# A graph network's node-group rows in f32 instead of f16, and the masks compared from them

## What is computed

```python
h = jnp.maximum(_layernorm(x), 0.0)
x = x + _L0_gnn_ref(h, src, dst, ...)              # GCN: segment_sum of x[src] * norm
h = jnp.maximum(_layernorm(x), 0.0)
x = x + _L1_gnn_ref(h, edge_index, W1, b1, W2, b2) # relu(relu([x_i, x_j - x_i] @ W1 + b1) @ W2 + b2), segment_max
h = jnp.maximum(_layernorm(x), 0.0)
x = x + _L2_gnn_ref(h, edge_weight, ...)           # segment_sum(h[src] * weight) / degree, two linear maps
h = jnp.maximum(_layernorm(x), 0.0)
x = x + _L3_gnn_ref(h, edge_index, edge_type_8, ...)  # two relational convolutions: two passes over the edges
```

## Time and profile before

| | us |
|---|---|
| median of 3 runs | 10746.02 |
| lowest and highest | 10732.53, 10749.62 |
| the profiled execution | 10738.4 |
| its span | 10736.3 |

### The profile page before, as it was taken

The page is one execution under the profiler, slowest core; times in us unless marked ns, Lnnn a source line. Parts: engine busy times, 40 slices in busy tenths (PEclk is TensorE's granted clock), DMA queues, the critical chain, the costliest instruction groups (busy, mean ns, idle before and its releaser), DMA issues.

```text
span 10736.3 us, 132836 instructions
## 1 busy us (share of the span) xinstructions
PE 5143.0 (48%) x35468; PEld 3759.8 (35%) x35468; DVE 4481.7 (42%) x9066; ACT 1867.5 (17%) x5090; POOL 6455.6 (60%) x6245
## 2 busy tenths in 40 slices
PE   3788477667676557777777311111112321111111
PEld 3677455555555435555555111111111111111110
DVE  7898555555555554444444221121112121111112
ACT  0677223323333200000000100000000100000000
POOL 8234555555555546666565566666666566666666
PEclk9999778888877778889888655555555655555555
DMA  6000133333333212222222222222221222222222
GB/s 260 23 15 15 36 88 95 93 92 94 93 92 92 79 44 65 64 63 64 65 64 62 82 58 56 56 57 59 56 58 56 87 58 56 57 56 58 57 58 56
DMA packets 501320, 736.15 MB, mean 69 GB/s; under 512 B 142419, under 2 KB 217811, under 8 KB 498372
## 3 DMA queue, kind: packets, MB, share of 16 engines
q0 software_dynamic: 199616, 212.17, 9.4%
q1 hardware_dynamic: 174060, 258.01, 7.7%
q10 hardware_dynamic: 127584, 265.22, 6.5%
HBM read 429.83 MB, written 305.03 MB: 68 GB/s over the span
## 4 chain that ended last, share of the span: by engine, by line
another core or an unknown queue 37%; PE 23%; issue 18%; DVE 11%; POOL 4%; DVEq 3%; ACT 2%; SPq 1%; DMA 1%; ACTq 0%; POOLq 0%
PE ps L1674 11%; DVE scn L1330 3%; PE ps L1738 2%; PE ps L1706 2%; PE ps L1583 2%; PE ps L1550 1%; POOL big L723 1%; PE ps L1555 1%; DVE picked_nodes L1266 1%; DVE idx L1292 1%; POOL big L786 1%; PE ps L1723 1%; PE ps L1649 1%; SPq L591 1%
## 5 line engine op out<-in xcount | busy, mean ns | idle before, releaser
L776 POOL DMA_INDIRECT gat<-typed_table,idx x3128 | 2996.7, 958 | 1591.4 <-issue 905.8
L776 POOL DMA_INDIRECT gat<-node_table,idx x2689 | 2626.6, 977 | 1845.0 <-issue 887.0
L1674 PE MATMUL ps<-big 128*128 128x320 bf16 x13230 | 2313.5, 331 | 627.3 <-issue 317.7
L1738 PE MATMUL ps<-ident,scn 128*128 128x128 f32 x3136 | 873.0, 370 | 3566.9 <-DVE scn L1330 2409.7
L1330 DVE TENSOR_TENSOR_SCAN scn<-flags,scn,ps 128x256 f32<-128x256 bf16 x1176 | 873.5, 743 | 3518.1 <-remote 3257.7
L1738 PEld LDWEIGHTS ps<-ident,scn 128*128 128x128 f32 x3136 | 533.5, 213 | 3869.6 <-issue 3847.2
L1674 PEld LDWEIGHTS ps<-big 128*128 128x128 bf16 x13230 | 1405.2, 109 | 1306.3 <-issue 450.9
L862 ACT COPY dmp<-ps 128x256 f32<-128x256 f32 x1568 | 578.9, 369 | 6295.8 <-remote 3966.9
L1706 PE MATMUL ps<-ident,gat 128*128 128x128 f32 x3136 | 820.9, 355 | 501.3 <-DVE gat L1297 310.7
L1266 DVE SCALAR_TENSOR_TENSOR picked_nodes<-node_ids,nodes_in_groups,ps 128x320 f32<-128x320 f32 x441 | 240.0, 544 | 1297.9 <-remote 749.3
L1706 PEld LDWEIGHTS ps<-ident,gat 128*128 128x128 f32 x3136 | 473.3, 177 | 646.0 <-issue 588.7
(11 more groups left out here) (289 smaller groups left out, 6037.9 us busy)
## 6 DMA issues: line engine op xcount, KB each, us to landing
scan_rows<-dmp ACTq DMA_DIRECT2D x784, 256.0 KB
flags<-keep_and_type_rows SPq DMA_DIRECT2D x980, 128.0 KB
spread_table<-tsl ACTq DMA_DIRECT2D x101, 576.0 KB, 16.0
shared<-spread_table SPq DMA_DIRECT2D x196, 288.0 KB
gat<-typed_table,idx POOLq DMA_INDIRECT x3128
gat<-node_table,idx POOLq DMA_INDIRECT x2689
typed_table<-shared SPq DMA_DIRECT2D x20, 1280.0 KB
group_rows<-node_group_rows SPq DMA_DIRECT2D x196, 128.0 KB
```

Of the source, the lines that this page charges most:

```text
L776: nc.gpsimd.indirect_dma_start(gat[:, k, g // ST, g % ST, :], None, table[:, :], bass.IndirectOffsetOnAxis(ap=idx[:, k, g:g + 1], axis=0)) ...
L1674: last = nc.tensor.matmul(product_bank(q, n), masks[:, n % 2, a, :], x3p[:, t, a, :, :].rearrange("p d b -> p (d b)"), start=a == 0 and t ...
L1738: last = nc.tensor.transpose(bank(2 + b1)[:, g * P:g * P + P], by_edge(scn[:, b1, :], g), ident[:, :])
```

## The change

The rows of node groups are held in f32: the table in DRAM (`group_d`), the tile into which SP loads (`grows`), and the tile that is written to the table (`group_t`). `grp_id` stays f16 and the masks stay bf16. To make room, `grp` no longer has memory of its own but lies over `scn`, the scan buffer, which is first written in the MLP pass; `group_t` lies there too. No instruction is added, removed or moved on any engine; L884 becomes a copy from f32 to f32.

```diff
-    group_d = nc.dram_tensor("node_group_rows", [NS, P], f16).ap()
+    group_d = nc.dram_tensor("node_group_rows", [NS, P], f32).ap()
...
-        grp = sb("node_groups", [P, NS])
...
-        grows = sb("group_rows", [P, K, P], f16)
+        grows = sb("group_rows", [P, K, P])
...
-        group_t = scn[:, :, :].rearrange("p b n -> p (b n)")[0:NS // 4, 0:2 * P].bitcast(f16)
+        grp = scn[:, :, :].rearrange("p b n -> p (b n)")[:, 0:NS]
+        group_t = scn[:, :, :].rearrange("p b n -> p (b n)")[0:NS // 4, 0:4 * P]
```

## The result

The changed kernel takes **10,770.3 us** (median of 11 runs, 10,756.5 to 10,785.2) beside 10,756.2 us for the kernel before, run beside it (11 runs, 10,732.5 to 10,769.2): ratio **1.0019**, 95% interval 1.0011 to 1.0026. A repetition (after_again) gave 1.0015 [1.0005, 1.0025]. In one set of runs used further down (set 3), one of 21 executions of the kernel before took 18,755 us; it is left out of the ratios.

What follows compares the result with a forecast made beforehand. Both passes were held bound by engines waiting for each other. Terms 101 + 68 + 50 + 35 + 30 = 284 us, less 20, on 10738 gave 11002, as a median 11,010 us; 8-in-10 range 10,870 to 11,135.

Steps and rivals of the forecast that it cites:

- The mask's price: DVE's mask comparison in both passes: 1500 ns with one f32 operand, +0.69 us each, 441 times.
- All 147 MLP masks on the path, +101: MLP pass: every mask releases PE's product, so each added 0.69 us counts, 101 us.
- 98 turns of the weighted pass, +68: Weighted pass: 98 masks lie between pick and scaling while PE idles, 68 us; the other 196 cost nothing.
- I take off 20 us: Whole sum: 20 us absorbed where PE waits for fetches or 4 to 6 us stalls without known cause.
- The clock, weighted +50: Weighted pass: longer PE idle time turns some 30 product pieces slow, 1.7 us each, 50 us.
- The clock, MLP +35: MLP pass: longer PE idle time turns about 22 product pieces slow, 1.6 us each, 35 us.
- The load, +30: MLP pass: masks for position 4 wait for loads grown to 256 KB, 0.8 us each, 30 us.
- Held fetches, put at 0: Both passes: longer masks hold POOL's fetches, perhaps 120 us more POOL time, costing 0 because POOL has room.
- A: Rival: idle DVE hides half of 169 us, no clock reaction; +85, 10,830 us; chance 0.17.
- B: Rival: the mask keeps its rate, only the load changes; 0 to 30 us, 10,755 us; chance 0.05.
- C: Rival: mask as fast as now and lets go of POOL, 49 us of held fetches return; 10,700 us; chance 0.02.
- D: Rival: slow clock lasts (+85 more), loads lengthen stalls or show as size (+100); 11,190 us; chance 0.10.

Runs made afterwards that it cites:

- set 3: Third of five sets of follow-up runs, each with the kernel before run beside it; there the kernel before took 10,767 us.
- few_f32: Changed kernel with all fetches but one of each step left out in both passes; one run, MLP pass 2286 us, weighted pass 1681 us.
- twice_both: Kernel before, with one f16 instruction making each mask twice in both passes; ratio 1.048 to the kernel before.
- mask_only: Kernel before with `grp_id` in f32, so masks are long; rows f16, loads 128 KB; ratio 1.0073.
- wtd_again: Kernel before with f32 rows in the weighted pass alone, f16 masks in the MLP pass; ratio 1.0149, where signals were on time.
- load_only: Kernel before with loads doubled to 256 KB and f16 masks; ratio 1.0004.
- few: Kernel before with all fetches but one of each step left out in both passes, f16 masks; one run, MLP pass 1998 us, weighted pass 1661 us.
- mlp_only: Kernel before with f32 rows used in the MLP pass alone; ratio 1.0087.
- gap_both: Kernel before with small POOL memsets behind the fetches of some steps, 196 in the weighted and 147 in the MLP pass; ratio 0.9975.
- pad_hold: Kernel before with an extra DVE comparison of 512 elements from two SBUF operands ahead of each f16 mask; ratio 1.0077.
- set 4: Fourth of five sets of follow-up runs; signals were on time and the kernel before took 9,308.6 us.
- half: Kernel before with all fetches but two of each step left out in both passes, f16 rows; one run, MLP pass 2005 us, weighted pass 1662 us.
- thrice_wtd: Kernel before, with one f16 instruction making each mask three times in the weighted pass alone; ratio 1.0357.
- short_f32_wtd: Kernel before with f32 rows in the weighted pass alone, each mask there made for 5 of 10 node groups; 9,307.4 us.

## Why the prediction was wrong, step by step

- **The mask's price: right.** 1.50 forecast, 1.479 measured, by the slope between rows of mixed operands.
- **All 147 MLP masks on the path, +101: right as PE's idle time wherever signals are on time** (+110 in few_f32, +97 in twice_both), wrong where they are late (+44 in the changed kernel).
- **98 turns of the weighted pass, +68: the same.** +65 in few_f32; in the changed kernel PE's idle time fell by 46. Gaps of PE of 4 us and more went from 33 (194 us) to 12 (79 us), all other gaps of 0.6 us and more from 206 to 270 us. The +64 is there, and the stalls gave back 115. (In mask_only they gave back nothing, and the pass was shorter by its busy time.)
- **The failed step: "I take off 20 us"** for the stalls without a cause. The terms ahead of it add up to 284 and the change measured 14, so with these terms it should have been 270. Some 60 us of that are the clock and 30 the load, below; the largest part is waiting: 169 us forecast at the masks, -2 us of idle time measured. I had seen the stalls and priced them by feeling. A stall whose cause is unknown makes every added time uncertain by its whole sum; here about 365 and 606 us of late signals stood against 304 us of new work. The prediction had named this sign itself: if the mask is long and a pass does not grow, another wait had been the last one there.
- **The clock, weighted +50: wrong in its reason.** From the earlier trace rows I read that an idle time of 2.7 us makes the next product slow. In few_f32 the idle time is 2.72 us, and the product runs at 2.4 GHz:

```profile
4235.83 0.41 PE L1716 MATMUL ps<-ident,gat 128*128 128x128 f32 x2 [2.72 <-DVE gat L1307]
4236.07 2.21 PE L1684 MATMUL ps<-big 128*128 128x320 bf16 x15
```

  In the whole weighted pass PE's busy time fell by 46 us there, and rose by 32 in wtd_again. The single idle time ahead of a product does not set its clock; my sorting mixed it with the stalls further back.
- **The clock, MLP +35: right in sign, five to six times too small** where signals are on time (busy +178 in few_f32 and +215 in twice_both, granted clock 0.95 to 0.84 and 0.83). In the changed kernel it was +15, from 0.81 to 0.79; that much of the slow running was there already is my reading.
- **The load, +30: wrong, 0.** load_only gives +5 and -3. The wait for the load grows to 140 us with 128 KB loads too, once other waits are gone (140.3 in few, 141.1 in twice_both).
- **Held fetches, put at 0: probably wrong without late signals.** The size was near: the fetches of the changed kernel take 162 us more of POOL's time in the weighted pass and 6 in the MLP pass, for the 120 of the prediction. In wtd_again a fetch that begins inside a mask lasts 2.14 us, and DVE then waits for its rows:

```profile
4339.45 1.46 DVE L1263 TENSOR_TENSOR big<-group_rows,group_ids 128x1280 bf16<-128x1280 f32 x1
...
4339.59 2.14 POOL L782 DMA_INDIRECT gat<-node_table,idx  x1 [0.30 <-issue]
...
4343.25 0.23 DVE L1299 COPY idx<-src_i 128x4 int32 x1 [2.34 <-DMA gat<-node_table,idx]
```

  The fetch ends 0.82 us behind the mask, as the earlier trace rows had it. PE's idle time in this pass grows by 104 us, 65 by the turns as in few_f32, and I put the other 39 down to this. That last split is an inference from two runs.
- **The rivals.** A (+85) had the right direction for the right reason, that cover exists, and named DVE's idle time instead of the stalls. B's 0 to 30 us holds the measured 14, but by luck: its condition, a mask that keeps its rate, did not come true. C's fetches were held longer, not let go. D (+440) has the size that twice_both measured, +448, and in part the reason: slower matmuls are 237 us of it (D had 170), while the loads and the unexplained stalls, for which D added 100, are not in it.

**What stays open.** Why signals are late in four of the five sets and in the first measurement, and on time in one, with the same program. Why a longer single comparison shortens the weighted pass where they are late: neither pauses of POOL behind a step nor the same time in two instructions does, and the longer fetches that come with it are not ruled out. Why the MLP pass pays 59 us in the changed kernel and 110 in mlp_only, whose MLP masks are the same. No run here tells.

## What to carry to other kernels

Before a wait is priced, sum up the idle time that no instruction of the program ends ("remote" in a one-core program, signals that come microseconds behind their work); if that sum is larger than the change, forecast two cases, one in which they cover the change and one in which they are not there. A cost of a change that was measured where such stalls rule says little of where they don't: here the edit is +0.2% in one case and, by the doubled masks, +4.8% in the other. A ratio below 1 needs the stretch named that got shorter: gap_both's passes are no shorter together than before, and its profile is shorter in stretches that the edit did not touch. And a run that is to stand in for a mechanism needs its dose and its place measured: pad_hold held the fetches by 60 us where the long mask holds them by 160.

## What the runs showed of the hardware

- The kernel before takes 9,309 us in one set of runs and 10,699 to 10,767 in the others, each set within 0.5%; two of these sets, one of either kind, carry the same chip number. The difference is in all passes over edges (MLP 355 us, weighted 371, typed 288 and 278) and goes with late semaphore updates of PE. In the first typed pass the delay sum is 2746 us before and 27 to 31 us in set 4.
- Where signals are late, cutting POOL's fetches from 26 to 16 in eight steps removes it (633 to 44 us in the weighted pass), and the typed passes of the same run, with all fetches, keep it (half: 2764 us in the first).
- is_equal on DVE, 1280 elements into bf16: 0.81 us from two f16 operands and 1.48 us with one f32 operand, whichever of the two it is (after, mask_only). 2560 elements from f16 take 1.48 (twice_both), 3840 take 2.15 (thrice_wtd), 640 with f32 0.81 (short_f32_wtd).
- A fetch that POOL issues during such a comparison mostly ends 0.82 us behind the comparison's end: 1.48 us beside a mask of 0.80 us (before), 2.14 beside one of 1.46 (wtd_again), where 0.94 is usual.
- PE's clock: few_f32's weighted pass has 98 idle times of PE, all but one of them 2.6 to 2.9 us long, at a granted clock of 0.98 on average.
